# Two block borders of a four-stage transformer kernel: last probability tiles turned by TensorE, MLP work drawn into the attention's end, a fourth bank for maxima, values without bias

## The chip, the cores and the metric

The kernel runs on one core of one Trainium2 chip. The metric is the device time of one execution in microseconds, as the median of a few runs.

## The reference, cut to what matters

A residual stream `x` of 2 x 1024 tokens and 256 channels goes through four sub-layers, each `x = x + layernorm(f(layernorm(x)))`, all in float32.

```
x = x + LN(attention0(LN(x)))   # 16 heads of 128, weights = FP4 codes * block scales, softmax over 1024 keys, bias bq bk bv bo
x = x + LN(mlp0(LN(x)))         # silu(x G^T * gs) * (x U^T * us) @ D^T * ds, inner width 704
x = x + LN(attention1(LN(x)))   # 16 heads of 16, causal, bias on q k v and on the projection
x = x + LN(moe(LN(x)))          # 16 experts, top 8, 2 shared
```

The change lies at the end of the first attention, in the start of the MLP, and in the start of the second attention.

## The kernel before

Each stage is a block in which the five engines run programs of their own, held together by semaphores; at a block's end all engines meet. Every product of two float32 tensors is done as three TensorE passes over a high part and a low part ("halves"): ScalarE rounds a tensor to its high half, GpSimd or VectorE subtracts it from the whole to give the low half. So nearly every operand costs a ScalarE copy and a subtraction. `xT` holds the normalised input transposed, in halves; `x` is the residual, `acc` the stage's output before its norm. PSUM has eight banks of 512 columns.

**First attention** (`attention0_stage`). Eight passes of two heads. A pass has 32 tiles (128 queries by 1024 keys). Work is laid out by slots: in slot `at`, TensorE computes the scores of tile `at+1`, a projection or output unit that falls due, and weighs the values with part `at-7`. VectorE takes each tile's maximum (L1098), ScalarE its exponential (L977). The probabilities have to be transposed: VectorE turns 32 x 32 blocks (L1104), SP stores the tile to DRAM (L699) and fetches it back with the blocks in their new places (L706) into `probT_lo`. Four tiles (a group) make four parts of 256 keys each by 512 queries; ScalarE makes a part's high half (`probT_take`, L987), GpSimd its low half in place (`split_lo`, L620), and TensorE weighs (`weigh`). In the last pass two of the last parts are split by VectorE. Per group the result `o` is split (L992, L1108), multiplied by the output weights (`output`, units 0 to 15, two per group) and summed into `acc` by VectorE (L1124).

In the last pass tables name the slots in which work for the next stage is issued: `STATS_ACC`, `NORM_ACC` (norm of `acc`), `ADD_X`, `NORM_X` (residual add, statistics, scale and offset on GpSimd at L216 to L221, and normalisation on ScalarE at L261 of the token groups 0 and 1), `TURN_X`, `TAKE_X` (its transposition by TensorE at L365 and its halves). `SCALE_MLP` and `FIRST_HI` prepare the MLP's first weight part.

**MLP** (`Mlp0.block`). Six weight parts by four token chunks of 512 are 24 steps. TensorE does `gate_up(s+1)` (12 products of 512 columns) and then `down(s)`; ScalarE the silu and the hidden high half, VectorE the product, GpSimd the hidden low half. Each weight part is loaded, scaled by VectorE and split in the early steps (`SPLIT`, step: part). Token groups 2 and 3 are normalised and turned in the same steps.

**Second attention** (`attention1_stage`). Steps of 128 keys by 512 queries for four heads. Before a step's scores, the row maxima come from separate products (`maxima`, L2105), which VectorE reduces (L2141): unit `g+11` in step `g`. They are numbered as fills, and fill `n` goes to bank `n % 3`; four banks form a ring for the scores and small jobs; bank 7 (`o_bank`) collects the weighed values. The block starts with step -6; the values of the first batch are projected in steps -6 to -3 (`take_v` on VectorE, L2703, adds a bias that is loaded when the block begins) and are placed by GpSimd (L2400). ScalarE's first exponentials come in step -2.

## Time and profile before

| | us |
|---|---|
| median of 3 runs | 1950.24 (1946.65 to 1952.3) |
| profiled execution, its own time | 1944.76 |
| its span, first to last instruction | 1943.0 |
| TensorE busy | 1855.7 (96%) |
| VectorE busy | 1431.3 (74%) |
| ScalarE busy | 1175.5 (60%) |
| GpSimd busy | 1169.9 (60%) |

The profile is one execution. Matmul durations overlap (a product of 512 columns shows 0.40 and the next starts 0.23 later). "PE" is TensorE, "PEld" its weight loads, "DVE" VectorE, "ACT" ScalarE, "POOL" GpSimd, "SP" the queue that issues the DMAs. The first attention runs from the start to 1134 us, the MLP to 1255, the second attention to about 1580, the experts to the end. "[3.83 <-POOL ...]" behind a row says that the engine idled for 3.83 us before it, until that work of GpSimd ended.

### The profile page before, as it was taken

The numbers are of one execution on the slowest core, as the hardware profiler recorded it, in microseconds if no ns is written. First come the engines' busy times: TensorE is split into PE (matmuls) and PEld (weight loads), VectorE is DVE, ScalarE is ACT, GpSimd is POOL, SyncE is SP. The second block draws the span as 40 slices with busy tenths as digits, with TensorE's granted clock in tenths as the row PEclk, the third lists the DMA queues.
The fourth block names the chain that finished last, engine by engine and source line by source line (L and its number), as shares of the span: only waits on it lengthen the run. The fifth ranks groups of instructions, "written<-read, shape, count | busy, mean of one in ns | idle before, by whom it ended". The sixth has DMA issues, their size and how long they took to land. (4 is left out here: it accounts for less than half of the span.)

```text
span 1943.0 us, 31274 instructions
## 1 busy us (share of the span) xinstructions
PE 1855.7 (96%) x10576; PEld 1463.3 (75%) x10576; DVE 1431.3 (74%) x2316; ACT 1175.5 (60%) x1901; POOL 1169.9 (60%) x945
## 2 busy tenths in 40 slices
PE   6999999999999999999999789989999989999997
PEld 5778888888888888888888578744555546888886
DVE  7778888888888788888888755487777766655556
ACT  5666666666666666766666655366666765533333
POOL 3676776777777767867766755224334446544345
PEclk9999999999999999999999899999999999999999
DMA  6877777778778777777787620000000010110001
GB/s 212 280 253 272 271 260 279 255 269 284 254 258 281 257 271 270 270 262 260 270 280 252 211 60 28 10 4 4 4 4 5 1 50 25 41 42 25 17 1 44
DMA packets 195603, 310.68 MB, mean 160 GB/s; under 512 B 12080, under 2 KB 154160, under 8 KB 195504
## 3 DMA queue, kind: packets, MB, share of 16 engines
q1 hardware_dynamic: 195504, 309.39, 46.3%
q8 instruction: 59, 0.97, 0.2%
q14 instruction: 40, 0.33, 0.1%
HBM read 173.03 MB, written 136.31 MB: 159 GB/s over the span
## 5 line engine op out<-in xcount | busy, mean ns | idle before, releaser
L620 POOL TENSOR_TENSOR attn_probT_lo<-attn_probT_lo,attn_probT_hi 128x1024 fp32r<-128x1024 f32 x254 | 610.3, 2403 | 199.1 <-ACT attn_probT_hi L987 198.7
L1104 DVE STREAM_TRANSPOSE attn_turned_prob<-attn_prob 128x1024 f32<-128x1024 f32 x256 | 318.0, 1242 | 127.8 <-ACT attn_prob L977 66.9
L977 ACT ACTIVATE attn_prob<-psum,attn_neg_max 128x1024 f32<-128x1024 f32 x256 | 285.6, 1116 | 147.6 <-DVE attn_neg_max L1098 144.6
L1098 DVE TENSOR_REDUCE attn_neg_max<-psum 128x1 f32<-128x1024 f32 x256 | 305.5, 1193 | 19.1 <-PE psum L81 18.9
L987 ACT ACTIVATE attn_probT_hi<-attn_probT_lo 128x1024 fp32r<-128x1024 f32 x256 | 269.1, 1052 | 3.1 <-DMA attn_probT_lo<-attn_spill 3.1
L81 PE MATMUL psum<-attn_probT_hi,attn_v_hi 128*128 128x512 f32 x512 | 206.4, 403 | 20.2 <-POOL attn_probT_lo L620 18.5
L81 PE MATMUL psum<-attn_probT_lo,attn_v_hi 128*128 128x512 f32 x512 | 205.7, 402 | 0.0
L81 PE MATMUL psum<-attn_key_hi,attn_q_hi 128*128 128x512 f32 x512 | 201.0, 393 | 3.4 <-ACT attn_prob L977 1.8
L81 PE MATMUL psum<-attn_probT_hi,attn_v_lo 128*128 128x512 f32 x512 | 204.1, 399 | 0.0
L81 PE MATMUL psum<-attn_key_lo,attn_q_hi 128*128 128x512 f32 x512 | 202.3, 395 | 0.0
L81 PE MATMUL psum<-attn_key_hi,attn_q_lo 128*128 128x512 f32 x512 | 201.7, 394 | 0.0
L2141 DVE TENSOR_REDUCE attn_peaks<-psum 128x1 f32<-128x512 f32 (+1 forms) x256 | 155.9, 651 | 44.4 <-PE psum L2112 29.8
L1765 POOL TENSOR_TENSOR attn_qk_lo<-attn_moe_hidden,attn_qk_hi 128x512 fp32r<-128x512 f32 (+1 forms) x73 | 93.5, 1282 | 142.9 <-ACT attn_qk_hi L1707 142.9
L2596 ACT ACTIVATE attn_probT<-psum 128x512 f32<-128x512 f32 (+1 forms) x256 | 129.2, 575 | 41.3 <-PE psum L2478 36.1
L830 POOL TENSOR_TENSOR attn_v_lo<-attn_v_whole,attn_v_hi 128x512 fp32r<-128x512 f32 x64 | 83.1, 1299 | 104.4 <-ACT attn_v_hi L999 104.2
L1794 DVE TENSOR_TENSOR attn_moe_hidden<-psum,attn_v 128x512 f32<-128x512 f32 (+1 forms) x73 | 49.8, 683 | 115.7 <-ACT attn_v L1700 109.0
L81 PEld LDWEIGHTS psum<-attn_probT_hi,attn_v_hi 128*128 128x128 f32 x512 | 97.4, 190 | 43.8 <-issue 12.7
L81 PEld LDWEIGHTS psum<-attn_key_hi,attn_q_hi 128*128 128x128 f32 x512 | 96.8, 189 | 28.8 <-ACT attn_prob L977 3.3
L81 PE MATMUL psum<-xT_hi,attn_w_hi 128*128 128x512 f32 x288 | 116.4, 404 | 0.8 <-DVE xT_lo L379 0.4
L2414 POOL TENSOR_SCALAR_AFFINE_SELECT attn_probT<-attn_probT 128x256 f32<-128x256 f32 x128 | 51.7, 417 | 108.4 <-ACT attn_probT L2596 56.3
L81 PEld LDWEIGHTS psum<-attn_probT_hi,attn_v_lo 128*128 128x128 f32 x512 | 97.2, 190 | 23.6
L81 PE MATMUL psum<-xT_hi,attn_q 128*128 128x512 f32 x288 | 114.6, 398 | 0.0
(259 smaller groups left out, 4740.3 us busy)
## 6 DMA issues: line engine op xcount, KB each, us to landing
attn_spill<-attn_turned_prob SPq DMA_DIRECT2D x256, 512.0 KB, 4.7
attn_probT_lo<-attn_spill SPq DMA_DIRECT2D x256, 512.0 KB, 5.1
x_sb<-in_w_qkvo SPq DMA_DIRECT2D x30, 512.0 KB, 5.0
attn_v_all<-in_moe_w SPq DMA_DIRECT2D x24, 384.0 KB, 3.0
acc_sb<-in_x SPq DMA_DIRECT2D x4, 512.0 KB, 6.0
acc_sb<-in_bo SPq DMA_DIRECT2D x16, 128.0 KB, 7.1
x_sb<-in_x SPq DMA_DIRECT2D x4, 512.0 KB, 5.4
mlp_staged<-in_ffn_w SPq DMA_DIRECT2D x4, 384.0 KB, 4.9
```

Source lines behind the costliest of these rows:

```text
L81: ins = nc.tensor.matmul(out, stationary[s], moving[m], start=start and n == 0, stop=stop and n == len(PASSES) - 1)
L620: engine.tensor_tensor(lo, f32(lo), f32(hi), ALU.subtract).then_inc(done, 1)
L830: nc.gpsimd.tensor_tensor(v[1][:, to, cols], v_whole[:, to, cols], f32(v[0][:, to, cols]), ALU.subtract).then_inc(v_done, 1)
L977: nc.scalar.activation(prob[:, tile % 2, :].rearrange("p (b n) -> p b n", b=NSQ), by_key, ACT.Exp, bias=neg_max[:, tile % 2:tile % 2 + 1], ...
L987: nc.scalar.activation(hi, f32(lo), ACT.Copy).then_inc(hi_done, 1)
L1098: nc.vector.tensor_reduce(neg_max[:, tile % 2:tile % 2 + 1], scores(tile), AX.XY, ALU.max, negate=True).then_inc(max_ready, 1)
L1104: nc.vector.transpose(turned_prob[:, tile % 2, :], prob[:, tile % 2, :]).then_inc(turned, 1)
L1765: self.nc.gpsimd.tensor_tensor(self.hid[1][p % 2][:, at], self.hidden[p % 2][:, at], f32(self.hid[0][p % 2][:, at]), ALU.subtract).then_in ...
L1794: self.nc.vector.tensor_tensor(self.hidden[p % 2][:, at], self.k.psum[:, self.slots[p % 2][1], at], self.gate_act[p % 2][:, at], ALU.mult) ...
L2141: nc.vector.tensor_reduce(to[:, h:h + 1], bank[:, 0:width], AX.X, ALU.max, negate=True).then_inc(max_free, 1)
L2414: nc.gpsimd.affine_select(out=at, in_=at, pattern=[[0, 2], [1, P]], compare_op=ALU.is_ge, fill=0.0, base=0, channel_multiplier=-1).then_in ...
L2596: nc.scalar.activation(probT[:, slot(g, h), q0:], score_bank(g, h), ACT.Exp, scale=float(D1) ** -0.5).then_inc(exp_done, 1)
```

## The change

1. *First attention's last tiles.* Tiles 30 and 31 of the last pass aren't turned, stored and fetched. Their exponential is written in key order; TensorE transposes them in eight 128 x 128 pieces into their own score banks (`flip`), VectorE copies these into `v_whole` in the layout of the parts (`take_flip`), ScalarE makes the high half of their 256 query columns from there, and VectorE the low half from PSUM (`flip_lo`). Parts 28 to 31 are therefore put together from two fetched tiles (two pieces per part on ScalarE and GpSimd) and two flipped ones. No part is split by VectorE as a whole any more.
2. *Order of the last slots.* The last four output units come in slots 37 to 40 and not 37, 39, 41, 43; the takes of parts 28 to 31 in slots 34 to 36; the norm work in later slots; the second token group is added and gets its statistics here, but is normalised and turned in the MLP.
3. *MLP.* The gate and up products of step 0 are done in the attention's end, and the halves of weight parts 0 and 1 (in the memory of the attention's q, k and v weights, `w_first`); parts 2 and 3 are loaded there into the memory of `turned_prob` (`parts_home`). These buffers lie on the other side of SBUF for all eight passes.
4. *Second attention.* Fills 16 to 35 go round four banks (0, 1, 2 and `o_bank`), later ones round three; the first batch's values are copied by ScalarE, later ones copied by VectorE, and the bias is added by GpSimd as it places them.

Below, in this order: tables, the loads on SP, GpSimd, TensorE, ScalarE and VectorE in the attention, then the MLP, then the second attention.

```diff
-    STATS_ACC, NORM_ACC, ADD_X, NORM_X = {25: 0, 28: 1}, {27: 0, 30: 1}, {31: 0, 33: 1}, {32: 0, 34: 1}
-    TURN_X, TAKE_X = {35: 0, 37: 1}, {36: 0, 38: 1}
-    SCALE_MLP, FIRST_HI = 34, 35
+    STATS_ACC, SCALE_ACC, NORM_ACC = {25: 0, 28: 1}, {25: 0, 28: 1}, {27: 0, 33: 1}
+    ADD_X, STATS_X, SCALE_X, NORM_X = {31: 0, 35: 1}, {31: 0, 36: 1}, {34: 0}, {36: 0}
+    TURN_X, TAKE_X = {37: 0}, {38: 0}
+    FIRST_PRODUCTS = {38: 0, 40: 1}
+    SCALE_MLP, FIRST_HI = 34, {36: 0, 40: 1}
+    FLIPPED = range(TILES - 2, TILES)
+    FLIP_AT, TAKE_FLIP = {30: (30,), 31: (31,)}, {30: (30,), 31: (31,)}
+    LAST_OUT = {37: 12, 38: 13, 39: 14, 40: 15}
+    LAST_TAKE = {34: (28,), 35: (29, 30), 36: (31,), 37: ()}
...
+            def load_rest():
+                for tile in range(TILES - len(FLIPPED) - 2, TILES - len(FLIPPED)):
+                    sp.wait_ge(stored[tile % STORES], passes * GROUPS * 16)
+                mlp.load_home(sp)
...
+                    if with_flips(m, part):
+                        for t in range(GT - len(FLIPPED)):
+                            hi, lo = tile_of_pair(part, t)
+                            ins = nc.gpsimd.tensor_tensor(lo, f32(lo), f32(hi), ALU.subtract)
+                        ins.then_inc(lo_done, 1)
...
-                if by_dve(m, part):
-                    pe.wait_ge(lo_done_dve, 1 + (part == PARTS - 1))
-                else:
-                    wait(pe, lo_done, m, PARTS, part + 1 - (1 if last(m) and part == PARTS - 2 else 0))
+                wait(pe, lo_done, m, PARTS, part + 1)
+                if with_flips(m, part):
+                    pe.wait_ge(flip_lo_done, part - (PARTS - GT) + 1)
...
+            def flip(tile):
+                pe.wait_ge(exp_done, (passes - 1) * TILES + tile + 1)
+                for kt in range(ST):
+                    mm = nc.tensor.transpose(scores(tile)[:, kt // GT, kt % GT * P:(kt % GT + 1) * P],
+                                             prob[:, tile % 2, kt * P:(kt + 1) * P], k.ident[:])
+                mm.then_inc(flipped, 1)
...
+                if last(m) and at in FIRST_PRODUCTS:
+                    mlp.first_product(pe, FIRST_PRODUCTS[at], after.lo_done, first_lo_done)
...
+                if with_flips(m, part):
+                    for t in range(GT - len(FLIPPED)):
+                        hi, lo = tile_of_pair(part, t)
+                        nc.scalar.activation(hi, f32(lo), ACT.Copy)
+                    act.wait_ge(flip_taken, len(FLIPPED))
+                    nc.scalar.activation(probT_hi[:, j, :, :, GT - len(FLIPPED):, :].rearrange("p k a t n -> p (k a) (t n)"),
+                                         flip_home[:, 2 * j:2 * j + 2, :, :, :].rearrange("p k a t n -> p (k a) (t n)"),
+                                         ACT.Copy).then_inc(hi_done, 1)
+                    return
...
+            def take_flip(tile):
+                dve.wait_ge(v_done, passes * V_PIECES)
+                dve.wait_ge(flipped, FLIPPED.index(tile) + 1)
+                for c in range(SEQ // NB):
+                    ins = nc.vector.tensor_copy(flip_home[:, c * GT:(c + 1) * GT, :, FLIPPED.index(tile), :],
+                                                scores(tile)[:, c, :].rearrange("p (k a n) -> p k a n", k=GT, a=NSQ))
+                ins.then_inc(flip_taken, 1)
+
+            def flip_lo(part):
+                dve.wait_ge(hi_done, (passes - 1) * PARTS + part + 1)
+                j = part % GT
+                for tile in FLIPPED:
+                    hi, lo = tile_of_pair(part, tile % GT)
+                    whole = scores(tile)[:, j // 2, j % 2 * 2 * P:(j % 2 + 1) * 2 * P].rearrange("p (k a n) -> p a k n", k=2, a=NSQ)
+                    ins = nc.vector.tensor_tensor(lo, whole, f32(hi), ALU.subtract)
+                ins.then_inc(flip_lo_done, 1)
...
+    def first_product(self, pe, which, x_done, w_done):
+        if which == 0:
+            pe.wait_ge(x_done, KC)
+            pe.wait_ge(w_done, 1)
+        first_col = which * self.cols_up
+        project(self.nc, self.k.psum[:, which, :],
+                lambda kt: [h[:, 0, first_col + kt * IM:first_col + (kt + 1) * IM] for h in self.first_halves],
+                lambda kt: [h[:, kt, 0:NB] for h in self.k.xT])
...
-        X_ADD, X_STATS, X_ACT, X_TURN = {3: 2, 7: 3}, {4: 2, 8: 3}, {5: 2, 9: 3}, {7: 2, 11: 3}
-        SPLIT = {-1: 1, 0: 2, 1: 3, 2: 4, 3: 5, 4: 0}
+        ACC_SCALE, ACC_ACT = {3: 2, 4: 3}, {4: 2, 5: 3}
+        X_ADD, X_STATS, X_ACT, X_TURN = {5: 2, 7: 3}, {6: 2, 8: 3}, {7: 2, 9: 3}, {2: 1, 8: 2, 11: 3}
+        SPLIT = {-1: 2, 0: 3, 1: 4, 2: 5}
...
-                gate_up(0)
                 for s in range(STEPS):
...
+        for fill in range(first_fill, HALVES * HALF_FILLS):
+            turn = fill - first_fill
+            bank = (0, 1, 2, sums_bank)[turn % 4] if fill < sums_fill else turn % MAX_BANKS
+            bank_of_fill[fill], fill_earlier[fill], had[bank] = bank, had.get(bank), fill
...
+                if g == 0:
+                    pe.wait_ge(max_free, last_in_sums_bank + 1)
...
+                if half == 0:
+                    pool.wait_ge(consts, 128)
-                    one[:].unsqueeze(2).unsqueeze(3).broadcast_to([P, ST, HG, D1]), ALU.mult).then_inc(v_ready, 1)
+                    own_bias.unsqueeze(1).broadcast_to([P, ST, HG, D1]), ALU.add).then_inc(v_ready, 1)
...
+                    if kind == "v" and of == 0:
+                        t = of * ST + 2 * part
+                        act.wait_ge(misc_full, use + 1)
+                        nc.scalar.activation(v_all[:, t:t + 2, :], misc_bank(use).rearrange("p (t n) -> p t n", t=2), ACT.Copy).then_inc(v_full, 1)
...
-                nc.vector.tensor_tensor(
-                    v_all[:, t:t + 2, :], misc_bank(use).rearrange("p (t n) -> p t n", t=2),
-                    bias_v[:].unsqueeze(1).broadcast_to([P, 2, C]), ALU.add).then_inc(v_full, 1)
+                nc.vector.tensor_copy(v_all[:, t:t + 2, :], misc_bank(use).rearrange("p (t n) -> p t n", t=2)).then_inc(v_full, 1)
```

## Rows read from the trace of the kernel before

**Rows 1.** The page's first part, busy us, share of the span and instructions.

```profile
PE 1855.7 (96%) x10576; PEld 1463.3 (75%) x10576; DVE 1431.3 (74%) x2316; ACT 1175.5 (60%) x1901; POOL 1169.9 (60%) x945
```

**Rows 2.** Table by stretches; the last three columns are granted clock, DMA share, GB/s.

```profile
core 0: us, PE busy (x) PEld busy (x) DVE busy (x) ACT busy (x) POOL busy (x), PEclk, DMA share, GB/s
...
1102.70:1134.80 32.10, 21.72 (x94) 16.87 (x94) 20.83 (x39) 14.12 (x20) 14.71 (x13) 0.81 0.08 27
1134.80:1139.30 4.50, 4.45 (x13) 3.56 (x14) 2.84 (x9) 1.53 (x2) 3.82 (x6) 0.62 0.76 246
1139.30:1255.30 116.00, 111.99 (x689) 91.36 (x687) 57.00 (x123) 62.44 (x105) 60.12 (x70) 1.00 0.09 28
1256.50:1276.40 19.90, 14.29 (x98) 10.19 (x98) 14.97 (x25) 4.62 (x7) 1.24 (x3) 1.00 0.14 22
```

**Rows 3.** Order of time, TensorE, attention's end: start, us, what, [idle before <- releaser].

```profile
1094.50 0.50 PE L81 MATMUL psum<-attn_probT_hi,attn_v_hi 128*128 128x512 f32 x1 [0.93 <-POOL attn_probT_lo L620]
...
1102.70 0.80 PE L81 MATMUL psum<-attn_probT_hi,attn_v_hi 128*128 128x512 f32 x1 [3.83 <-POOL attn_probT_lo L620]
...
1109.95 0.77 PE L81 MATMUL psum<-attn_probT_hi,attn_v_hi 128*128 128x512 f32 x1 [3.04 <-POOL attn_probT_lo L620]
...
1119.06 1.04 PE L365 MATMUL psum<-ident_sb,acc_sb 128*128 128x128 f32 x8
...
1134.85 0.53 PE L81 MATMUL psum<-xT_hi 128*128 128x512 f32 x1 [1.99 <-PEq L1173]
...
1139.28 0.39 PE L81 MATMUL psum<-xT_hi,mlp_w_hi 128*128 128x512 f32 x1
```

**Rows 4.** The same view of VectorE.

```profile
1097.34 1.25 DVE L1104 STREAM_TRANSPOSE attn_turned_prob<-attn_prob 128x1024 f32<-128x1024 f32 x1 [1.27 <-ACT attn_prob L977]
1100.73 0.69 DVE L1108 TENSOR_TENSOR attn_o_lo<-psum,attn_o_hi 128x512 fp32r<-128x512 f32 x1 [2.15 <-ACT attn_o_hi L992]
1101.34 0.86 DVE L1124 SCALAR_TENSOR_TENSOR acc_sb<-psum,attn_over_total,acc_sb 128x256 f32<-128x256 f32 x2
1102.12 1.60 DVE L275 TENSOR_TENSOR x_sb<-x_sb,acc_sb 128x1024 f32<-128x1024 f32 x1
...
1107.81 3.07 DVE L275 TENSOR_TENSOR x_sb<-x_sb,acc_sb 128x1024 f32<-128x1024 f32 x1
...
1132.17 1.66 DVE L1124 SCALAR_TENSOR_TENSOR acc_sb<-psum,attn_over_total,acc_sb 128x256 f32<-128x256 f32 x4 [0.34 <-PE psum L81]
```

**Rows 5.** The same view of ScalarE.

```profile
1096.11 1.11 ACT L977 ACTIVATE attn_prob<-psum,attn_neg_max 128x1024 f32<-128x1024 f32 x1 [1.47 <-DVE attn_neg_max L1098]
...
1107.54 2.08 ACT L261 ACTIVATE acc_sb<-x_sb,room_sb 128x256 f32<-128x256 f32 x4 [5.89 <-POOL room_sb L221]
1109.52 1.99 ACT L987 ACTIVATE attn_probT_hi<-attn_probT_lo 128x1024 fp32r<-128x1024 f32 x2
```

**Rows 6.** The same view of GpSimd.

```profile
1094.71 2.38 POOL L620 TENSOR_TENSOR attn_probT_lo<-attn_probT_lo,attn_probT_hi 128x1024 fp32r<-128x1024 f32 x1 [0.26 <-ACT attn_probT_hi L987]
...
1105.67 0.24 POOL L216 TENSOR_SCALAR room_sb<-room_sb 128x4 f32<-128x4 f32 x1 [3.03 <-DVE room_sb L256]
...
1110.63 2.48 POOL L620 TENSOR_TENSOR attn_probT_lo<-attn_probT_lo,attn_probT_hi 128x1024 fp32r<-128x1024 f32 x1 [0.83 <-ACT attn_probT_hi L987]
...
1163.12 0.74 POOL L1458 TENSOR_TENSOR mlp_hid_lo<-mlp_hidden,mlp_hid_hi 128x256 fp32r<-128x256 f32 x1
```

**Rows 7.** The same view of the DMA queue: issue of the last fetches.

```profile
1098.99 4.44 SPq L706 DMA_DIRECT2D attn_probT_lo<-attn_spill  x2
```

**Rows 8.** The same view, start of the second attention, VectorE and ScalarE.

```profile
1263.05 0.69 DVE L2703 TENSOR_TENSOR attn_v_all<-psum,attn_bias_v 128x512 f32<-128x512 f32 x1 [2.40 <-DMA attn_bias_y<-in_b_proj]
1263.88 2.57 DVE L2141 TENSOR_REDUCE attn_peaks<-psum 128x1 f32<-128x512 f32 x4
...
1263.67 0.69 ACT L2118 ACTIVATE attn_qk_hi<-psum,attn_bias 128x512 fp32r<-128x512 f32 x1 [7.34 <-PE psum L81]
...
1276.32 3.60 ACT L2596 ACTIVATE attn_probT<-psum 128x512 f32<-128x512 f32 x8
```

More of the change, by code:

```diff
@@ L353, in normalise_x, with normalise_x_half @@
             self.normalise(self.k.acc if self.x is None else self.x, g, self.x_normed)
+    def normalise_x_half(self, act, g, half):
+        if half == 0:
+            act.wait_ge(self.x_ready, g + 1)
+        for t in self.tiles(g)[half * GT // 2:(half + 1) * GT // 2]:
+            ins = self.nc.scalar.activation(self.k.acc[:, t, :], self.x[:, t, :], ACT.Identity, bias=self.offset[:, t:t + 1],
+                                            scale=self.rstd[:, t:t + 1])
+        if half:
+            ins.then_inc(self.x_normed, 1)
     def banks(self, g):
@@ L477, in wait @@
             eng.wait_ge(sem, value)
+    last = lambda m: isinstance(m, int) and m == passes - 1
+    first = lambda m: isinstance(m, int) and m == 0
     def qk_unit(slot):
@@ L493, in v_unit, with out_unit @@
         return 4 * (half + V_AT[i][0]) + V_AT[i][1]
-    def out_unit(slot):
+    def out_unit(m, slot):
+        if last(m) and slot >= min(LAST_OUT):
+            return LAST_OUT.get(slot)
         for part in range(2):
@@ L504, in uses_of @@
         found = []
-        for kind, unit, per_pass in (("qk", qk_unit(slot), QK), ("out", out_unit(slot), OUTS), ("v", v_unit(m, slot), V)):
+        for kind, unit, per_pass in (("qk", qk_unit(slot), QK), ("out", out_unit(m, slot), OUTS), ("v", v_unit(m, slot), V)):
             if unit is not None and there(m, unit, per_pass):
@@ L614, in part_pair, with tile_of_pair @@
             return probT_hi[:, j, :, :, :, :].rearrange("p k a t n -> p (a t) k n"), lo
-        by_dve = lambda m, part: isinstance(m, int) and m == passes - 1 and part in (PARTS - 3, PARTS - 1)
+        flip_home = v_whole[:].rearrange("p t d -> p (t d)").rearrange("p (k a t n) -> p k a t n", k=ST, a=NSQ, t=len(FLIPPED))
+        def tile_of_pair(part, t):
+            group, j = part // GT, part % GT
+            lo = probT_lo[:, group % 2, :, t, 2 * j:2 * j + 2, :]
+            return probT_hi[:, j, :, :, t, :].rearrange("p k a n -> p a k n"), lo
         def split_lo(engine, part, done):
@@ L620, in split_lo @@
             engine.tensor_tensor(lo, f32(lo), f32(hi), ALU.subtract).then_inc(done, 1)
+        flips = lambda m, tile: last(m) and tile in FLIPPED
+        with_flips = lambda m, part: last(m) and part >= PARTS - GT
         def each_slot(eng, slot):
@@ L630, in each_slot @@
                 slot(passes - 1, at)
-        last = lambda m: isinstance(m, int) and m == passes - 1
-        first = lambda m: isinstance(m, int) and m == 0
         def v_split_at(m, at):
@@ L723, in exchange @@
                     for t in tiles[:3]:
-                        store(m, t)
+                        if not flips(m, t):
+                            store(m, t)
                         between(m, t)
@@ L854, in _ @@
             each_slot(pool, slot)
[L855 removed]
+            mlp.first_lo(pool, first_hi, first_lo_done)
+            after.scale_x(pool, 1)
         @block.tensor
@@ L947, in slot @@
                     weigh(m, at - WEIGH_AT)
+                for tile in FLIP_AT.get(at, ()) if last(m) else ():
+                    flip(tile)
                 if last(m) and at in TURN_X:
                     g = TURN_X[at]
+                    pe.wait_ge(flip_lo_done, GT)
                     after.turn(pe, g, last_turn_banks(g)).then_inc(after.turned, 1)
+                if last(m) and at in FIRST_PRODUCTS:
+                    mlp.first_product(pe, FIRST_PRODUCTS[at], after.lo_done, first_lo_done)
             pe.wait_ge(consts, 3 * 16)
@@ L1019, in slot @@
             def slot(m, at):
-                part = at + 1 - WEIGH_AT
-                if there(m, part, PARTS):
-                    probT_take(m, part)
+                for part in LAST_TAKE.get(at, (at + 1 - WEIGH_AT,)) if last(m) else (at + 1 - WEIGH_AT,):
+                    if there(m, part, PARTS):
+                        probT_take(m, part)
                 if (at - KEEP_AT) % GT == 0 and there(m, (at - KEEP_AT) // GT, GROUPS):
@@ L1128, in slot @@
             def slot(m, at):
-                if there(m, at, TILES):
+                if there(m, at, TILES) and not flips(m, at):
                     turn_prob(m, at)
+                for part in LAST_TAKE.get(at, ()) if last(m) else ():
+                    flip_lo(part)
                 if (at - 5) % GT == 0 and there(m, (at - 5) // GT, GROUPS):
@@ L1144, in slot @@
                     (take_qk_lo if kind == "qk" else take_v if kind == "v" else add_up)(m, unit)
-                part = at + 1 - WEIGH_AT
-                if there(m, part, PARTS) and by_dve(m, part):
-                    dve.wait_ge(hi_done, (passes - 1) * PARTS + part + 1)
-                    split_lo(nc.vector, part, lo_done_dve)
+                for tile in TAKE_FLIP.get(at, ()) if last(m) else ():
+                    take_flip(tile)
                 if last(m):
@@ L1312, in gate_up @@
                     wait_slot(pe, ("step", s))
-                    early_halves = e == 0 and c == 0
-                    if not early_halves:
+                    if e in splits_before:
                         pe.wait_ge(w_ready, splits_before[e] + 1)
```

166 lines of the change are left out of this document (100 added, 66 removed).

## The prediction

> **What bounds the kernel now.** I read the page's busy times first: TensorE is busy 96% of the span, no other engine over 74% [rows 1]. So only a stretch in which TensorE stands, or runs at its low clock, can give time back. The table by stretches finds two [rows 2]: the end of the first attention (1102.7 to 1134.8 us: 21.7 busy of 32.1 at a granted clock of 0.81, and 0.62 over the MLP's first 4.5), and the second attention's first 20 us (14.3 of 19.9). Between them the MLP is bound by TensorE (112.0 of 116.0). All parts of the change lie in these two stretches. The order of time then says who is late.
>
> *End of attention.* The last score product ends at 1093.6 (the product at 1094.50 less its 0.93 of idle time); TensorE then waits 3.8 and 3.0 us for GpSimd's split of a part of the probabilities [rows 3]. GpSimd is late because it holds, between two splits, for VectorE's statistics of the first residual group (3.03 idle until 1105.67 [rows 6]), and works its scale and offset before the next split; ScalarE stands behind the same chain for 5.89 us and takes two parts at 1109.52 [rows 5]. The round trip through DRAM of the last tile (turned by 1098.6, stored, last fetch issued behind that store, by 1103.4 [rows 4, 7]) is over before ScalarE comes to it: it is the second wait, hidden by the first. The MLP then starts after 2.0 us of block change with low-clock products [rows 3].
>
> *Start of the second attention.* VectorE is the bound: 15.0 busy of 19.9 [rows 2]; it takes the maxima and the values, and stands 2.40 us for the bias that is only loaded when the block begins; ScalarE idles 7.34 [rows 8], and its first exponentials start at 1276.32.
>
> **The change, part by part: the attention's end.** From the last score on I lay the new order out by the old durations (times on the clock of the profiled execution).
> - Tile 30 isn't turned by VectorE, so the last maximum starts behind the score at 1093.6 and not behind the 1.25 us transposition: done at 1094.8, its exponential (1.11 [rows 5]) at 1095.9, against 1097.2.
> - TensorE: six products of a part are 1.4 us, an output unit 0.7, eight transpositions 1.04 [rows 3]. Part 23 (starts 1094.5), flip of tile 30 to 1097.0; output, part 24, flip of tile 31 to 1100.2.
> - GpSimd: without the statistics between them the splits of parts 24 to 27 run back to back from 1094.7 at 2.38 each [rows 6]: 1104.3 (before: the last of them, 1110.63 and 2.48, ended at 1113.1). Parts 28 to 31 are now two pieces of 256 columns, 0.74 each [rows 6]: 1.5 per part; with one scale and offset (from 1105.67 to the old next split, 1.8) between them they end at 1112.2.
> - ScalarE: a whole part is 1.0 [rows 5]; three pieces instead of one cost two starts more, 0.2 each as estimate, 1.4; with a normalisation of 2.06 before them, part 31 is taken by 1109, the residual's normalisation and the Silu table then end by 1112.5. Ahead of need.
> - VectorE carries most of the new work and is the last stretch's bound. No trace shows its copy out of PSUM into runs of 32 columns; the nearest row is the split of o out of PSUM, 0.69 for 512 [rows 4], and a transposition of 1024 is 1.25. Bounds for 512: 0.6 (half of that) and 1.25 (runs of 32 cost double); I take 0.67, by the split, which reads such runs too. Its late splits (256 columns out of PSUM) stand nearest to the output sums, 0.43 each [rows 4]; bounds 0.35 to 0.8. So: flip copies of tile 30 to 1098.4; o and sums 1.55; flip copies of 31 from 1100.2 to 1101.6; residual add 1.60 and statistics 1.8 (between the add's end, 1103.7, and GpSimd's release) to 1105.0; sums 0.86; late split 28 to 1106.8; weight rows 1.1 (two of 256, as sums with a neighbour's split); late splits 29, 30 to 1109.6; o and sums 1.55 to 1111.2; second residual add 3.07 to 1114.2; late split 31 to 1115.1; statistics 1.8; two sums 1.7; the low half of the turned x, 1024 columns, 1.2, to 1119.8. TensorE then has the MLP's first product, two output units and the second product: 1.4 + 1.4 + 1.4 = 1124.0. The block change adds 1.0 (sums ended 1133.8, the MLP began at 1134.8 [rows 3, 4]): the MLP starts at 1125 instead of 1134.85.
>
> Of these the second residual add is the dearest: 3.07 beside a GpSimd split, 1.60 where less of one ran [rows 4]. The Trainium skill ("SBUF — State Buffer", Who interferes with whom) says that VectorE and GpSimd share one port pair as an exclusive lock, taken also by a VectorE operation with two SBUF inputs, and the loser waits for the whole instruction. By that rule the new flip copies and late splits, which read PSUM, wait for nobody, while the first add would now also fall under a running split and cost up to one split more, 2.4 us; the end would be 1127 rather than 1125. The row of 3.07 agrees.
>
> **The MLP's start.** The two first projections (12 products) are gone from it: its first work is now what began at 1139.28 [rows 3], so 1139.28 - 1125 = 14.3 us. Against it: they ran at the low clock (granted 0.62 [rows 2]), 4.43 us instead of 2.8, and I let the same 1.65 fall on the next 12 products; and the turn of the second x group moves from the attention's idle time into the MLP, where nothing hides it: 1.04 on TensorE. 14.3 - 1.65 - 1.04 = 11.6. Its ScalarE and VectorE work, the halves of the normalisation and the later acc pieces lie under the MLP's products (ScalarE 62 and VectorE 57 busy of 116 [rows 2]). On GpSimd the split of part 2 (768 columns, 1.8, between 0.74 for 256 and 2.38 for 1024 [rows 6]) now comes before the first hidden half: at most 0.8 us for TensorE, covered while the clock is low. The loads of parts 2 and 3 are queued on SP only behind the last fetch, with nothing behind them. The loads of parts 4 and 5 land some 5 us into the block and are wanted in its second step of 4.2. I put nothing.
>
> **The second attention's start.** The bias wait (2.40) and four value evictions (0.69 each) leave VectorE, some 5.7 us with the free signals; the fourth bank lets TensorE write a pair of maxima while the pair before is read. Then TensorE is the bound up to its first score product, by the column rates of the products above: 8 pairs at 0.45, 4 values at 1.55, one projection 1.45, two pairs of stackings 1.3 = 12.5 from 1256.8 on, 1269.3; VectorE needs 16 maxima at 0.64 [rows 8] and 1.8 of other work = 12.1. ScalarE has the two last stackings and the table load left: its first exponentials start at 1272.3 instead of 1276.32: 4.0 us. Bounds: 1.5 (VectorE still ahead of it all, but without the bias wait's half) and 5.7. The values' bias moves to GpSimd, an add of the same 1.04 us as the product with one; it wants the bias at about 1270, and the old wait ended with its landing at 1263.05. The later values on VectorE, a copy for an add: nothing. The wait of the first weighing for the fourth bank is met a step before.
>
> **Sum.** 11.6 + 4.0 = 15.6; some 20 hand-offs between engines in the new chains at 0.03 to 0.1 us take 1.5: 14.1 us off. Profiled, 1944.76 (span 1943.0) goes to 1930.7. The median of the runs is 1950.24, 5.5 above the profiled one; 14.1 off it gives 1936.
>
> **Rivals.** *(B) VectorE in the attention's end costs more.* If the runs of 32 columns double the flip copies and late splits (+2.7 and +3.4), and the first residual add takes as long as the second (+1.5), the MLP starts at 1133 with its products done, 8 us later: about 6 off in all, 1944. For: VectorE is on the whole last chain. Against: the transposition, o and by-query reads with runs of 32 show no such cost, 0.69 for 512. *(C) Only the second attention gains*, because the first's end is set by something that I left out: 4 off, 1946. *(D) Slower: the clock.* In the two stretches before the MLP's steady part the granted clock was 0.81 and 0.62: some 8 us of full-clock time lost [rows 2]. If the many short stops of 0.5 to 1.5 us in the new end keep TensorE at 1.2 GHz, its 22 us of products within 30 take 44, 13.6 longer: all of the gain. Every us more at that level costs 0.5; with 13 of them in the MLP's dense part the kernel is 6 slower: 1956. It decides from the point where the low stretch outlasts the attention's end. For: the low stretches of before began right behind stops of 1.9 and 3.8 us. Against: with dense work after 1139.3 it was back at 1.00 at once, and the longest stop that I forecast, for late split 31, is 2.3. *(E) Nothing outside changes*: buffers move in SBUF over all eight passes; no row shows a dependence on place.
>
> **Chances.** Forecast 0.62 (1929 to 1941), B 0.22 (1940 to 1946), C 0.08, D 0.05, others 0.03. 0.3%, 5.9 us, is what a measurement of this kernel tells from no change. Faster by more: 0.62 + 0.17 of B's + 0.02 = 0.81; same: 0.13; slower: 0.06. Range: down to 1928 (no hand-offs 1.5, the MLP begun at the full clock 1.65, 5.7 at the second place 1.7, and the 3.6 by which the lowest run of before lies under the median), up to 1946 (C).
>
> **What would show it.** The MLP's first silu begins at 1125 (wrong if over 1129); no TensorE stop over 2.5 us between 1093 and 1124; GpSimd's four whole splits back to back from 1094.7; VectorE's flip copies near 0.67 and late splits near 0.43; the last 8 us of the attention led by VectorE. In the second attention, exponentials start 16 us after the block and not 20, with TensorE's stops for the maxima gone. The forecast fails if low-clock time grows, or if the MLP's steady part takes over 118 us.

## The result and the profile after

The changed kernel takes 1928.91 us (median of 4 runs, 1925.46 to 1933.36) against 1951.18 beside it (1946.65 to 1952.3): ratio 0.9883, 95% interval 0.9865 to 0.99, 22.3 us less. The forecast was 14.1 less and 1936, the range 1928 to 1946. Two executions of the experiments were slow ones, one of only_bias (9346 us) and one of the kernel before beside it (7642 us), and the ratios leave them out.

The profiled execution took 1925.46 with a span of 1923.8. First the page's busy times, then the table by stretches of the kernel after (the columns are those of [rows 2]).

```profile
PE 1848.3 (96%) x10592; PEld 1463.3 (76%) x10592; DVE 1424.8 (74%) x2320; ACT 1177.6 (61%) x1912; POOL 1170.9 (61%) x950
```

```profile
1102.70:1120.00 17.30, 14.04 (x73) 10.86 (x72) 15.29 (x40) 12.47 (x25) 14.10 (x16) 1.00 0.07 28
1120.00:1125.00 5.00, 3.88 (x23) 3.16 (x22) 2.05 (x6) 0.45 (x1) 3.72 (x7) 1.00 0.00 0
1125.00:1240.00 115.00, 111.63 (x696) 91.51 (x694) 59.50 (x131) 64.70 (x110) 58.17 (x73) 1.00 0.09 31
```

```profile
1241.00:1261.00 20.00, 17.01 (x116) 12.68 (x117) 13.55 (x23) 9.13 (x15) 1.90 (x4) 0.91 0.14 22
```

Busy shares hardly moved; the stretches did. The end of the first attention, 32 us at a clock of 0.81 before and then 4.5 at 0.62 [rows 2], is 22 us at 1.00, and the MLP's start carries no low clock. In the second attention's start TensorE does more (17.0 of 20, 14.3 before) but at 0.91, where it was 1.00.

The order of time on TensorE shows what is left of the waits of 3.83 and 3.04 us [rows 3]:

```profile
1097.19 1.03 PE L967 MATMUL psum<-ident_sb,attn_prob 128*128 128x128 f32 x8
...
1106.44 0.50 PE L81 MATMUL psum<-attn_probT_hi,attn_v_hi 128*128 128x512 f32 x1 [1.58 <-POOL attn_probT_lo L648]
...
1111.19 0.50 PE L81 MATMUL psum<-attn_probT_hi,attn_v_hi 128*128 128x512 f32 x1 [0.98 <-POOL attn_probT_lo L877]
...
1124.57 0.47 PE L81 MATMUL psum<-xT_hi,mlp_w_first_hi 128*128 128x512 f32 x1 [1.12 <-PEq L1263]
```

The same view of GpSimd, which answers to [rows 6]: four whole splits back to back, then the pieces.

```profile
1095.89 10.50 POOL L648 TENSOR_TENSOR attn_probT_lo<-attn_probT_lo,attn_probT_hi 128x1024 fp32r<-128x1024 f32 x4 [0.27 <-ACT attn_probT_hi L1056]
1106.35 1.43 POOL L877 TENSOR_TENSOR attn_probT_lo<-attn_probT_lo,attn_probT_hi 128x256 fp32r<-128x256 f32 x2
...
1109.72 5.21 POOL L877 TENSOR_TENSOR attn_probT_lo<-attn_probT_lo,attn_probT_hi 128x256 fp32r<-128x256 f32 x6
```

VectorE, against [rows 4]: flip copies, late splits, and the two residual adds.

```profile
1098.33 1.29 DVE L1180 COPY attn_v_whole<-psum 128x512 f32<-128x512 f32 x2 [2.35 <-PE psum L967]
...
1102.53 1.62 DVE L275 TENSOR_TENSOR x_sb<-x_sb,acc_sb 128x1024 f32<-128x1024 f32 x1
...
1106.75 0.75 DVE L1190 TENSOR_TENSOR attn_probT_lo<-psum,attn_probT_hi 128x256 fp32r<-128x256 f32 x2
...
1111.03 1.21 DVE L275 TENSOR_TENSOR x_sb<-x_sb,acc_sb 128x1024 f32<-128x1024 f32 x1
...
1121.43 1.66 DVE L1211 SCALAR_TENSOR_TENSOR acc_sb<-psum,attn_over_total,acc_sb 128x256 f32<-128x256 f32 x4 [1.81 <-PE psum L81]
```

### The profile page after: what moved, and what is told of

Same layout as the page of the kernel before. It is cut to its first block and busy times, and to the rows that moved or that the text cites. A ratio compares the mean times of both kernels' runs of the same rounds, so it can differ in the third digit from the quotient of the medians.

```text
span 1923.8 us, 31317 instructions
## 1 busy us (share of the span) xinstructions
PE 1848.3 (96%) x10592; PEld 1463.3 (76%) x10592; DVE 1424.8 (74%) x2320; ACT 1177.6 (61%) x1912; POOL 1170.9 (61%) x950
## 5 line engine op out<-in xcount | busy, mean ns | idle before, releaser
L1174 DVE STREAM_TRANSPOSE mlp_parts_home<-attn_prob 128x1024 f32<-128x1024 f32 x254 | 315.8, 1243 | 129.9 <-ACT attn_prob L1036 64.9
L1168 DVE TENSOR_REDUCE attn_neg_max<-psum 128x1 f32<-128x1024 f32 x256 | 305.5, 1193 | 19.7 <-PE psum L81 19.6
L1056 ACT ACTIVATE attn_probT_hi<-attn_probT_lo 128x1024 fp32r<-128x1024 f32 x252 | 265.0, 1052 | 2.2 <-DMA attn_probT_lo<-attn_spill 1.7
L81 PE MATMUL psum<-attn_probT_hi,attn_v_hi 128*128 128x512 f32 x512 | 204.3, 399 | 11.6 <-POOL attn_probT_lo L648 10.5
L81 PE MATMUL psum<-xT_hi,mlp_w_first_hi 128*128 128x512 f32 x288 | 116.0, 403 | 2.4 <-PEq L1263 1.1
L81 PE MATMUL psum<-xT_hi,mlp_w_first_lo 128*128 128x512 f32 x288 | 114.7, 398 | 0.0
```

The source lines that it names most:

```text
L81: ins = nc.tensor.matmul(out, stationary[s], moving[m], start=start and n == 0, stop=stop and n == len(PASSES) - 1)
L1056: nc.scalar.activation(hi, f32(lo), ACT.Copy).then_inc(hi_done, 1)
L1168: nc.vector.tensor_reduce(neg_max[:, tile % 2:tile % 2 + 1], scores(tile), AX.XY, ALU.max, negate=True).then_inc(max_ready, 1)
L1174: nc.vector.transpose(turned_prob[:, tile % 2, :], prob[:, tile % 2, :]).then_inc(turned, 1)
```

## How the executions are laid side by side

Four moments cut every profiled execution: the start of the last maximum on VectorE (a), the MLP's first DMA issue (b), the second attention's (c), and its first exponential (d). "Clock" is the mean granted clock of the 20 us from c on. The last column is the median of all runs of the kernel, with its ratio to the kernel before on the same chip.

| kernel | a to b | b to c | c to d (clock) | us, ratio (95%) |
|---|---|---|---|---|
| before | 39.9 | 121.8 | 19.7 (1.00) | 1951.2 |
| after | 29.8 | 117.0 | 17.5 (0.91) | 1928.9, 0.9883 (0.9865 to 0.99) |
| attn1_only | 40.4 | 123.2 | 18.6 (0.84) | 1948.5, 0.9982 (0.9961 to 1.0003) |
| tail_only | 30.0 | 117.1 | 19.7 (1.00) | 1932.1, 0.9899 (0.988 to 0.9918) |
| no_flip | 36.6 | 116.8 | 18.8 (0.84) | 1942.9, 0.9954 (0.9937 to 0.997) |
| first_in_mlp | 30.0 | 121.0 | 16.1 (0.97) | 1937.7, 0.9927 (0.9907 to 0.9948) |
| scale_early | 36.2 | 117.0 | 17.6 (0.86) | 1932.8, 0.9921 (0.9891 to 0.995) |
| after_again | 30.0 | 117.0 | 18.9 (0.84) | 1930.3, 0.9894 (0.9868 to 0.9921) |
| trimmed | 30.0 | 117.2 | 16.1 (0.95) | 1931.4, 0.9898 (0.9873 to 0.9923) |
| three_banks | 30.0 | 117.0 | 17.8 (0.96) | 1931.4, 0.9896 (0.9873 to 0.992) |
| values_dve | 29.8 | 117.0 | 18.2 (0.92) | 1933.1, 0.9909 (0.9887 to 0.9931) |
| only_bias | 29.8 | 117.0 | 19.9 (0.91) | 1935.0, 0.9925 (0.9903 to 0.9947) |
| trim_end | 29.9 | 117.0 | 17.5 (0.92) | 1930.8, 0.989 (0.9871 to 0.9909) |
| trim_both | 30.0 | 117.0 | 17.5 (0.91) | 1929.9, 0.989 (0.9873 to 0.9907) |

The 20 us of the clock column reach past d, so a low clock in them need not lie between c and d. From c to d alone the granted clock was 1.00 in before, tail_only, trimmed, first_in_mlp and three_banks, 0.90 or 0.91 in after, scale_early, values_dve, only_bias, trim_end and trim_both, and 0.83 or 0.84 in after_again, attn1_only and no_flip. The changed start of the second attention takes 16.1 at 1.00, 17.5 to 17.6 at 0.90 and 18.6 to 18.9 at 0.83 or 0.84.

With the changed code a to b and b to c repeat within 0.2 us from one execution to the next (with the code of before within 0.5 and 1.4); whole executions of the changed kernel lie up to 12 us apart (1922.61 to 1934.82). So the columns decide, and the medians only where the difference is large. The kernels after, after_again and trimmed are one and the same kernel: trimmed was meant to be an altered version, but the kernel that ran was the changed one as it is, and its expectation is judged on nothing.

> The changed kernel once more, with more runs, as the yardstick for the three kernels beside it and for the spread. Theory A (what it gains beyond the 16 us at the border and some 3.6 in the second attention is luck with low-clock spells of TensorE in the second attention): its runs lie between 1925 and 1936 us and go with their mean granted clock, about 1.9 us for each 0.001, median near 1930. Rival B (it has fewer such spells by its build): all runs near 1926 at a granted clock of 0.992.

> A version meant to be better than the changed kernel: GpSimd's scale and offset of the first token group come one part later (behind its pieces of part 29 and not of part 28), so that they aren't in front of the part that TensorE waits 0.98 us for; ScalarE makes the high half of weight part 1 in slot 37 and not 40, so that GpSimd splits it in its idle 2.94 us and its last scale and offset end by 1121; VectorE scales part 2 in slot 38 instead of behind the last sums. Theory A (TensorE's chain sets the attention's end, GpSimd and VectorE end with it by chance): the stop before part 29 goes and half of it comes back before part 30; last maximum to MLP start 29.0 to 29.4 us against 29.8, whole kernel 0.5 to 1 us faster, within the runs' spread. Rival B (GpSimd's total work sets it: it still has the same 28 us to do from 1094.7 on): 29.8 as before. Rival C (the later scale makes the normalisation, the Silu table and the turned x late): 30.5 to 31.5, with a TensorE stop of over 1.5 us before the first MLP product.

Measured for after_again: runs from 1923.56 to 1934.82, median 1930.3, at clocks of 0.987 to 0.994. Theory A holds but for its lowest run and its slope (below); rival B is out.

## Experiments: the two places apart

**attn1_only** is the kernel before with the second attention of the changed one, **tail_only** the reverse.

```
attn1_only:  before, up to "def attention1_stage"; from there the changed kernel
tail_only:   changed kernel, up to "def attention1_stage"; from there before
```

> The kernel before with the second attention of the changed kernel alone (four banks for the first maxima, values copied by ScalarE, bias added by GpSimd). Theory A (the two borders add up, each read from its own rows): the second attention's first exponentials come 17.5 us after its block begins instead of 19.7, 2.2 us less, and the kernel takes 2 to 4 us less than the kernel before; the first attention's end and the MLP stay as they were. Rival B (most of the 19 to 22 us come from the second attention, through fewer low-clock spells in it): 7 us or more less, with the granted clock between 1300 and 1580 us at 0.99 and not 0.97.

> The changed kernel with the second attention of the kernel before: only the first attention's end and the MLP are changed. Theory A: the second attention's block begins 15 us earlier than in the kernel before, and the kernel takes 15 to 17 us less. Rival B: under 12 us less, since the rest of the gain lies in the second attention.

Measured: 3.9 and 20.2 us less than before (medians 1948.47 and 1932.14 against 1952.36). The interval of attn1_only, 0.9961 to 1.0003, reaches 1: its medians alone don't show a gain. In its one profile c to d is 1.1 shorter (18.6, at a clock of 0.84 from c to d; expected 17.5), while a to b and b to c, whose code is that of before, are 0.5 and 1.4 longer. In tail_only the second attention begins 15.7 earlier, as theory A has it (15), but the median falls by more than its 15 to 17. The sum, 24.1, is a little over the 22.3 and 21.4 of the two together. So the attention's end and the MLP's start carry nearly all of it, and more than the 10.1 that I had forecast there (11.6 less 1.5 for hand-offs); the second attention gives what was forecast or less.

## Experiments: the attention's end

**no_flip**: no tile is turned on TensorE; the round trip through DRAM is back, the new order of work stays.

```diff
-    FLIPPED = range(TILES - 2, TILES)
-    FLIP_AT, TAKE_FLIP = {30: (30,), 31: (31,)}, {30: (30,), 31: (31,)}
+    FLIPPED = ()
+    FLIP_AT, TAKE_FLIP = {}, {}
```

> The changed kernel without the flips: tiles 30 and 31 go through DRAM again, parts 28 to 31 are whole parts on ScalarE and GpSimd; the new slots of the norm work, the takes, the outputs and the MLP's first products stay. Theory A (the stops of the kernel before came from GpSimd and ScalarE held behind the residual's statistics, the DRAM round trip was hidden behind that): the fetched tiles land near 1107.5, part 28 is taken 4 us later than with flips (1103.4), and the MLP starts 3 to 5 us later: 4 us slower than the changed kernel, about 15 faster than the kernel before its second attention counted. Rival B (the DRAM round trip of the last tiles was the bound of the end): the MLP starts 8 us or more later, over 8 us slower than the changed kernel.

Measured: a to b 36.6, so 6.8 longer than with the flips, between the two expectations, and only 3.3 shorter than before; the median is 9.5 under before, where after_again's is 21.4 under it. ScalarE's order of time in no_flip:

```profile
1107.51 2.95 ACT L1054 ACTIVATE attn_probT_hi<-attn_probT_lo 128x1024 fp32r<-128x1024 f32 x3 [4.36 <-DMA attn_probT_lo<-attn_spill]
```

TensorE in the same execution:

```profile
1111.17 0.47 PE L81 MATMUL psum<-attn_probT_hi,attn_v_hi 128*128 128x512 f32 x1 [1.81 <-POOL attn_probT_lo L647]
1116.00 0.80 PE L81 MATMUL psum<-attn_probT_hi,attn_v_hi 128*128 128x512 f32 x1 [2.34 <-POOL attn_probT_lo L647]
```

As soon as ScalarE no longer stands for the statistics, it stands 4.36 us for the fetched tiles, until 1107.51, the very time at which it got free before (1107.54 [rows 5]). In the kernel before the two waits were nearly tied: there the last fetch, issued at 1103.1, landed 3.9 us later, at 1107.0.

Not all of the 6.8 is the round trip. Counted from a, TensorE begins part 28 1.8 us later than with the flips (1111.17 here, 1108.66 in the trace of after), but part 31 6.5 later. In between GpSimd splits whole parts again, 2.4 us each instead of two pieces of 0.73, and stops of TensorE come with a low clock (0.81 from a to b, 1.00 in after). What each of the three takes was not separated.

**scale_early** puts GpSimd's scale and offset of the first token group back to where they wait for VectorE's statistics, as before.

```diff
-    ADD_X, STATS_X, SCALE_X, NORM_X = {31: 0, 35: 1}, {31: 0, 36: 1}, {34: 0}, {36: 0}
+    ADD_X, STATS_X, SCALE_X, NORM_X = {31: 0, 35: 1}, {31: 0, 36: 1}, {31: 0}, {36: 0}
```

> The changed kernel with one entry of a table moved back: GpSimd makes scale and offset of the first residual group in slot 31 as in the kernel before (behind the split of part 25, waiting for VectorE's statistics) and not in slot 34. Theory A (this wait held the splits, and with them TensorE, in the kernel before): GpSimd idles 4 to 5 us until the statistics end near 1105.9, the split of part 26 starts near 1107.7 and not 1101, TensorE stops for 4 us or more and falls to its low clock there, the MLP starts 4 to 6 us later. Rival B (the end is led by VectorE, GpSimd has slack): the MLP starts less than 1.5 us later.

Measured: a to b 36.2, 6.4 longer, the upper end of theory A or a little more. The median shows only 2.5 of it (1932.8 against 1930.3), which lies within the spread of the runs behind b; the profiled execution is 6.0 longer than that of after. GpSimd's row in scale_early:

```profile
1104.95 0.24 POOL L216 TENSOR_SCALAR room_sb<-room_sb 128x4 f32<-128x4 f32 x1 [5.24 <-DVE room_sb L256]
```

TensorE's in the same execution:

```profile
1109.51 0.76 PE L81 MATMUL psum<-attn_probT_hi,attn_v_hi 128*128 128x512 f32 x1 [6.91 <-POOL attn_probT_lo L648]
```

GpSimd's idle 5.24 us come out on TensorE as one stop of 6.91. So either one alone, the flips taken away or GpSimd's wait put back, takes back 6.4 to 6.8 of the 10.1 that a to b gained: the flips are worth little without this entry of the new order, and the order little without the flips. Part of both is the clock: from a to b it was 0.91 in scale_early and 0.81 in no_flip, against 0.83 before and 1.00 in after.

**first_in_mlp** does the first gate and up products at the MLP's start again, their weights ready.

```diff
-    FIRST_PRODUCTS = {38: 0, 40: 1}
+    FIRST_PRODUCTS = {}
 (and gate_up(0) again before the MLP's steps)
```

> The changed kernel with the MLP's two first projections back at the start of the MLP's block; all else as changed. Theory A (they were drawn into stops of TensorE, but the end is led by VectorE): the attention ends some 1.5 us earlier (the second projection, 1.4, is the last thing on TensorE there), the MLP begins with 12 products, 2.8 us at the full clock or 4.4 at the low one, and in sum the kernel is 1.5 to 3 us slower than the changed one. Rival B (they hide nothing, they only changed place): same time within 0.5 us. Rival C (what the move brought is the clock: without them TensorE stops longer at the border and the MLP begins at the low clock): 3 us slower or more, with a granted clock near 0.62 in the block's first 4.5 us.

Measured: a to b 30.0, the same as with them; b to c 121.0, 4.0 longer. The first product of the MLP in first_in_mlp:

```profile
1124.79 0.77 PE L81 MATMUL psum<-xT_hi,mlp_w_first_hi 128*128 128x512 f32 x1 [3.18 <-PEq L1263]
```

The table of its first 5 us, same columns as above:

```profile
1124.80:1129.80 5.00, 5.00 (x15) 4.01 (x16) 0.59 (x2) 1.42 (x2) 1.14 (x4) 0.67 0.78 243
```

The products cost nothing in the attention's end. Without them TensorE stands 3.18 us over the block's change and not 1.12, and works at 0.67 behind it: the twelve products take 4.4 us (1124.79 to 1129.19) instead of 2.8, and 0.4 comes back in the next step. That is rival C; theory A's earlier end of the attention did not come. The median is 7.4 over after_again's (1937.69 and 1930.3), more than is placed here.

**trim_end** and **trim_both** were meant to beat the changed kernel.

```diff
-    SCALE_MLP, FIRST_HI = 34, {36: 0, 40: 1}
+    SCALE_MLP, FIRST_HI = 34, {36: 0, 37: 1}
 (and mlp.scale_third behind after.take_lo in slot 38; trim_both also:)
-    ADD_X, STATS_X, SCALE_X, NORM_X = {31: 0, 35: 1}, {31: 0, 36: 1}, {34: 0}, {36: 0}
+    ADD_X, STATS_X, SCALE_X, NORM_X = {31: 0, 35: 1}, {31: 0, 36: 1}, {35: 0}, {36: 0}
```

> The changed kernel with two steps of the attention's last 10 us earlier: ScalarE makes the high half of weight part 1 in slot 37 and not 40, so that GpSimd splits it in its idle 2.94 us, and VectorE scales part 2 in slot 38 instead of behind the last sums. (The run trimmed turned out to hold the changed kernel itself, unaltered.) In the trace of the changed kernel GpSimd, VectorE and TensorE all end at 1123.4. Theory A (TensorE and the sums behind it set the end): GpSimd ends by 1121, VectorE 0.4 earlier, last maximum to MLP start 29.3 to 29.6 us against 29.8 and 30.0. Rival B (the two have to end for the block's change, and each was late by itself): 28.9 to 29.2. Rival C (the high half in slot 37 gets in front of the turned x on ScalarE): 30.2 to 30.8. Whole kernel within 0.5 us of the changed one but for the spread of the runs.

> As trim_end, and GpSimd's scale and offset of the first token group one slot later: behind its pieces of part 29 and not of part 28, so that they aren't in front of the part that TensorE waits 0.98 us for. Theory A (TensorE's chain sets the end): the stop before part 29 goes, 0.98, and half of it comes back before part 30; last maximum to MLP start 28.8 to 29.1, whole kernel 0.5 to 1 us faster than the changed one, within the runs' spread. Rival B (GpSimd's sum of splits sets it, whatever their order): as trim_end. Rival C (the later scale makes the normalisation, the Silu table and the turned x late): 30.0 to 31.5, with a stop of TensorE of over 1.5 us before the first MLP product.

Measured: 29.9 and 30.0; neither is better. In trim_end GpSimd's last work ends 2.7 us earlier behind a (26.0 against 28.7), and GpSimd then stands 3.83 until the block changes:

```profile
1123.91 0.52 POOL L1564 MEMSET mlp_zeros<- 1x512 f32 x1 [3.83 <-POOLq L1263]
```

So GpSimd and VectorE only ended together with TensorE's chain, which alone sets the end: theory A's cause, without its gain of 0.2 to 0.5. In trim_both the stop of 0.98 before part 29 is gone and comes back, larger, before part 30:

```profile
1114.97 0.50 PE L81 MATMUL psum<-attn_probT_hi,attn_v_hi 128*128 128x512 f32 x1 [1.55 <-POOL attn_probT_lo L877]
```

GpSimd's sum of splits bounds these parts, whatever their order: rival B.

## Experiments: the second attention's start

**three_banks** takes the fourth bank away again, **values_dve** gives the first values back to VectorE (as copies; the bias stays with GpSimd), **only_bias** does both, so that only the bias wait is gone.

```diff
three_banks:
-            bank = (0, 1, 2, sums_bank)[turn % 4] if fill < sums_fill else turn % MAX_BANKS
+            bank = turn % MAX_BANKS
values_dve:
-                    if kind == "v" and of == 0:
+                    if False:
-                    elif kind == "v" and of:
+                    elif kind == "v":
```

> The changed kernel with three banks for the maxima throughout; values still copied by ScalarE, bias still added by GpSimd. The mark is the time from the second attention's block start to its first exponentials: 19.7 us in the kernel before, 17.5 changed (16.1 where the clock stayed up). Theory A (once VectorE is relieved, three banks make TensorE stop for single maxima): 1.5 to 2 us later than with four banks, 18 to 19.5, with TensorE stops of 0.5 to 0.8 behind maxima again. Rival B (the relief of VectorE is everything, the bank nothing): as changed within 0.3.

> The changed kernel with the first batch's values copied by VectorE, as the later ones, and not by ScalarE; four banks, no bias wait. Same mark. Theory A (VectorE is again the bound with 2.7 us more on it): 2 to 2.5 us later than changed, 18.5 to 20, VectorE busy all through. Rival B (the wait for the bias was the whole cost, the engine that copies is indifferent): as changed within 0.5.

> The changed kernel with three banks for all maxima and with the first batch's values copied by VectorE and not by ScalarE: of the second attention's start only the bias wait (2.40 us of VectorE before) is gone from its front. Theory A (the bias wait is the largest of the three parts; bank and engine are worth about 1 us each): from the block's start to the first exponentials 18.3 us at a clock of 0.97 to 1.00 (19.7 before, 16.1 with all three), up to 1 more where the stretch's granted clock is under 0.92; whole kernel 2 us over the changed one, which the runs can hardly tell. Rival B (each of the three edits alone is enough, since VectorE only has to lose its lead once): 16.1 to 17. Rival C (the bias wait was hidden by other waits of VectorE): 19 to 20 at a full clock.

Measured from c to d: 17.8 at a clock of 0.96, 18.2 at 0.92, 19.9 at 0.91. They can only be read beside executions of the changed start with the same clock between c and d (see under the table): 16.1 at 1.00, 17.5 at 0.90. Three banks at 1.00 cost 1.7 (17.8 against 16.1), which is theory A's size. VectorE's copies at 0.91 cost 0.7 (18.2 against 17.5), between theory A (2 to 2.5) and rival B (0.5). Both together at 0.91 cost 2.4 (19.9 against 17.5), which is 1.7 and 0.7. Of the 3.6 between 19.7 and 16.1 the bias wait is left with 1.2, of its 2.40. So the three add up, and the bank is the largest of them, not the wait, as my theory A for only_bias had it; by its numbers (18.3, up to 1 more at a low clock) 19.9 is a miss too, since the low clock costs 1.4 there. Three banks, the copies and both together stand on one execution each. What the bank is worth can be seen on TensorE in three_banks, in a stop that the changed kernel doesn't have there:

```profile
1244.48 0.51 PE L2219 MATMUL psum<-attn_key,attn_q 64*128 64x512 f32 x2 [0.78 <-DVE attn_peaks L2255]
```

## Why the prediction was right, and where it missed

*The mechanism.* Right, with both signs of it tested: GpSimd's splits run back to back from 1095.89 to 1106.4, the silu of the MLP starts at 1124.55 (forecast 1125), no stop of TensorE over 1.6 us lies in the attention's end (forecast none over 2.5), and the flips and the order are both needed for it (no_flip, scale_early). One statement beside it was wrong: the round trip was called over by 1103.4 and hidden. 1103.4 is the end of the last issue [rows 7]; the data of that fetch landed at 1107.0, and in no_flip 3.7 us behind the issue's end (1103.8 to 1107.5). It was almost as late as the first wait (1107.54), and so the flips were needed for the gain.

*Durations.* Flip copies 1.29 for two, 0.645 each (0.67 taken); late splits 0.37 (0.43 taken, 0.75 for two); first residual add 1.62 (1.60). Runs of 32 columns cost nothing here: in values_dve VectorE's copy of 512 unbroken columns out of PSUM took 0.68. So rival B is out. GpSimd's add of the bias took 1.28, not 1.04. The second residual add took 1.21, not 3.07: the largest single miss of the VectorE chain, 1.9. The rows say what its price is made of:

```profile
1101.79 1.22 DVE L275 TENSOR_TENSOR x_sb<-x_sb,acc_sb 128x1024 f32<-128x1024 f32 x1
```

```profile
1103.02 3.37 POOL L648 TENSOR_TENSOR attn_probT_lo<-attn_probT_lo,attn_probT_hi 128x1024 fp32r<-128x1024 f32 x1
```

The first is scale_early's first residual add, while GpSimd idles: 1.22. Wherever a split or a piece runs on GpSimd as the add begins, the add ends 1.1 us behind that instruction's end. So it took 3.07 where 1.99 of a split was left, 1.60 to 1.64 where 0.52 to 0.55 was left, 1.67 where 0.59 of a piece was left (trim_both), and 1.21 where 0.11 was left (after). The second row, from after, is the split that GpSimd began under the first add: 3.37 instead of 2.4; of the six pieces five took 0.73 and the one beside the second add 1.73. By the rule of the Trainium skill ("SBUF — State Buffer", Who interferes with whom) the one that comes second waits until the other's instruction is over. The rows agree. The 3.07 was the price of an add that begins early under a whole split, and I put it where only pieces run. That the first add cost 1.62, and not up to 2.4 more, is luck of the moment: it began 0.54 before a split's end.

*The last stretch.* It is not led by VectorE, as I wrote, but by TensorE's chain with VectorE's sums behind it (1.81 idle on VectorE before its last sums; trim_end). The result is the same because both were laid out to the same end: from a to b it took 29.8 where 31.4 were laid out (1093.6 to 1125), from a start that in this execution lay 1.1 later.

*The MLP's start: the step that failed.* "I let the same 1.65 fall on the next 12 products", and 1.04 for the turn of the second x group. b to c is 117.0, where these terms make 120: 3 us of the miss. The low clock didn't come. It was 1.00 from 1102.7 on, where TensorE never stood longer than 1.6 us, and 1.00 in the MLP's first 5 us in all eleven executions whose first products lie in the attention's end. first_in_mlp shows the opposite case: with 3.18 us of standing the clock is 0.67 behind it. The turn is there, 0.8 us to the next product, but stops of 0.51 and 0.32 that the MLP of before had in its first 24 us are gone: its steady part shows 3.4 us without TensorE work in 115 against 4.0 in 116 [rows 2]. I had seen the low clock in the rows, but taken it as something that stays with the first dense work, and not as something that a stop brings and that may go with it. Rival D was this mechanism with the wrong sign.

That the stop alone decides is not shown. In attn1_only, with the MLP of before, TensorE stood 2.01 us at the same border, and the clock behind it was 1.00 (first 4.5 us, columns of [rows 2]):

```profile
1134.80:1139.30 4.50, 4.50 (x19) 3.54 (x20) 3.59 (x10) 2.12 (x3) 3.83 (x6) 1.00 0.81 246
```

There the first twelve products took 2.8 and not 4.43, and yet TensorE stood 1.23 and 0.79 us in the next two steps, and b to c was 123.2, longer than the 121.8 with the low clock. So what the low clock really cost the kernel before is open, and with it how the 4.8 us from b to c divide between the moved products (2.8 at the full clock) and the rest.

*The second attention.* 4.0 forecast; in the three profiles of the changed kernel 2.2, 0.9 and 3.6, at clocks of 0.90, 0.83 and 1.00 from c to d. The exponentials start 16.1 to 18.9 us after the block. The step was sized nearly right at full clock; what was not in it is the clock: from c to d it is low in nine of the twelve kernels that have at least one part of the new start, and 1.00 in the two that have none (before, tail_only). Part of the gain is lost to that. The cause is open: TensorE stands as long or longer at this border in those two (1.52 us, against 1.37).

*The sum.* From the program's start to b the changed code takes 1124.4 (mean of ten executions, no_flip and scale_early left out) against 1134.8: 10.4 earlier, 9.85 forecast. To c it takes 1241.3 (first_in_mlp left out too) against 1257.3 (mean of before and attn1_only): 16.0, where 11.6 less most of the 1.5 for hand-offs was forecast. From c to d 0.9 to 3.6. Together 16.9 to 19.6 are placed. The three medians of the one kernel give 22.3, 21.4 and 19.0. What lies over the placed part isn't assigned to an edit: from d to the experts' first load, the three executions of that kernel take 301.4, 303.7 and 310.2 us (304.1 before), at clocks of 0.99, 0.98 and 0.94 (0.97). The median of 1928.91 lies 0.9 inside the range; in the profiled execution 2.7 us of the gain come from this stretch (301.4 against 304.1), which no step of the forecast had. That part is luck.

## What to carry to other kernels

A low clock seen behind a stop may go with the stop; don't carry it over to the work that comes next. Behind stops of 1.99 [rows 3] and 3.18 us at the block's change the next twelve products took 1.6 us more each time, behind those of 1.0 to 1.1 nothing in eleven executions; but behind 2.01 in attn1_only nothing either, so one trace doesn't tell. Two waits that end at the same time must be taken away together, and an experiment with one of them back tells more than the total. A price taken from a row under contention is about the work alone plus what was left of the instruction in the way: VectorE's add took 3.07 with 1.99 of a GpSimd split left, and with pieces of 256 on GpSimd it can wait for 0.74 at most.

## What the runs showed that I had not expected

The runs of one kernel follow the mean granted clock: trimmed took 1922.61 at 0.994 and 1931.64 at 0.988, trim_end 1924.2 at 0.995 and 1934.26 at 0.987, some 1.4 us for each 0.001. Most of the low spells lie in the second attention and fall in other places in each execution. Even the same stop has no fixed answer: near 1083 us all fourteen profiles show TensorE standing 1.90 to 1.92 us for a split of GpSimd; the granted clock fell within 1.4 us behind it in nine of them, and stayed at 1.00 in the other five. What decides where the low spells fall was not tried.
